# A ViT tower on one core: in the joined attention and routing stage, projections split into two rounded parts, ranks in one pass, and the steps of a chunk in another order

## Chip, core and metric

The kernel runs on one core of a Trainium2 chip, as one launch. The time is the device time of that core in microseconds (us). The core has five engines with instruction queues of their own, which work in order and meet at semaphores: TensorE (PE; its weight loads are shown apart as PEld), VectorE (DVE), ScalarE (ACT), GpSimd (POOL), and SyncE (SP), which only issues transfers. TensorE's clock is granted at one of two levels, 1.2 or 2.4 GHz; the profile gives it as a share, 1.00 or 0.50.

## The reference, cut to the part that the change touches

Five layers follow each other: token attention, gated linear attention, a mixture of experts, a second attention, a feed-forward net. Tokens are 4 x 3136 = 12544 rows of D = 192. The change lies in the second layer and in the routing half of the third:

```python
q = (elu(x @ Wq) + 1) * M ** -0.5          # M = 64; x is the layer-normed h
k = elu(x @ Wk) + 1
v = x @ Wv                                 # 192 x 192
log_f = log(clip(sigmoid(x @ Wf + bf), 1e-6))
log_f_cum = clip(cumsum(log_f, axis=1), -20, 20)
cum_kv = cumsum(exp(-log_f_cum)[..., None] * k[..., None] * v[..., None, :], axis=1)
numerator = einsum('blm,blmd->bld', q, exp(log_f_cum)[..., None] * cum_kv)
denominator = einsum('blm,blm->bl', q, exp_pos * cumsum(exp_neg * k, axis=1)) + 1e-6
h = h + layernorm(numerator / denominator) @ Wo
# experts: on layernorm(h)
routing = softmax(gelu(x @ w1 + b1) @ w2 + b2)      # 8 experts
topv, topi = top_k(routing, 2)                      # each row goes to two experts
```

## The kernel before

The tokens are worked in **chunks** of 448 rows (CH), each of four tiles of 112 rows (T, TPC = 4); there are NC = 28 chunks, seven to an image. `attend_route_phase` is the joined stage. One program loop over g = 0 to 30 carries four chunks at different depths: chunk g is attended to, chunk g+1 is projected, chunk g-1 gets its statistics, g-2 goes through the router's net, and g-3 gets its places in the experts' rows. The order of each engine is the order in which its block calls small functions, written out by hand; nothing else schedules it.

What one loop does for a chunk:

- **Into the attention.** ACT normalises four tiles into `xn` (`normalise`); PE transposes them into the PSUM tile `ptr` (`transpose_x`); DVE copies that to `xT` (`take_x`), 96 rows in two pieces. PE multiplies with the forget weights into `pff` and with query and key weights into `pqk` (`project`), and gives the values in `pvo` (`values`). These matmuls are f32, and each stands in the trace as two records.
- **Gates.** DVE takes `pff` (`gate_in`) and `pqk` (`elu_in`), ACT does exp, ln and the exp of the elu (`gate`), DVE scans (`scan`, which gives `cum`), ACT takes the exponential of `cum` (`decay`), and DVE makes `qt` and `kt` from it (`q_and_k`). With that the next chunk's loop can start.
- **Attention.** PE makes scores in `pat` and turns the keys into `pff` (`weights`); DVE masks them to `at` (`mask_weights`), ACT copies `ktok` (`keys_out`). In `attend` PE does three matmuls for each tile, the state `pst` among them, which ACT copies to `snap` (`states`). DVE divides (`sums_out`), takes statistics (`sums_stats`, `sums_aggr`), POOL makes the reciprocal root `rst` by a power (`factor`), PE transposes `hh` and multiplies with `wo` (`transpose_n`, `wo_out`), and DVE adds to `h` (`add_out`, which waits for `rst`), then the bias and the next norm's statistics (`add_bias`, `take_stats`; POOL: `factor_route`).
- **Routing.** ACT writes `xr` (`normalise_route`), PE transposes it (`transpose_r`), multiplies (`router`), ACT does the Gelu between two table loads (`take_hidden`), PE gives logits (`logits`), DVE and ACT the softmax (`softmax_head`, `take_ex`), DVE picks two experts (`choose`). PE counts in `rank` how many rows before each one went to its expert, with six f32 matmuls of 8 to 32 columns into the bank of `pqk`. DVE makes row numbers of it (`places`) and the gates (`share`). POOL writes each row to two places in HBM with eight indirect transfers (`scatter`), out of a ring of three `xr`.

`map_tiles` stands after the last loop and gives SP the ends of the experts' regions; SP then fills eight blocks of 448 rows with zeros, behind the semaphore `map_out`. The stage `tile_phase`, which reads these rows, begins when all engines and transfers of the joined stage are through.

During loops 0 and 1 ACT and DVE also split the experts' down weights in two (`high`, `split_low`).

Of the kernel before, what the change touches and what calls it, by code (L numbers as in the profile page):

```python
# [17 lines left out]
D = 192  # L18
# [24 lines left out]
E = 8  # L43
# [510 lines left out]
def attend_route_phase(nc, ins, h, bns, mean, rstd, minus, eye, held, gate, slot, shift, tile_e, tile_r, down,  # L554
# [3 lines left out]
    V1 = D + 1  # L558
    G3 = 3
    with ExitStack() as ctx:  # L560
        sb, ps, sem = allocator(nc, ctx, held)
        wqk = sb("wqk", [KC, 2, 128])
        wff = sb("wff", [KC, 2, 128])
        bff = sb("bff", [128, 1])
        wv = sb("wv", [KC, 2, D])
# [10 lines left out]
        xn = sb("xn2", [T, TPC, D])  # L576
        xT = sb("xT2", [KC, 2, CH])
# [21 lines left out]
        earlier = sb("before3", [T, T])  # L599
        number = sb("number3", [T, E])  # L600
        region = sb("region3", [T, E])
# [15 lines left out]
        sel = sb("sel3", [T, TPC, E])  # L617
# [10 lines left out]
        past = sb("past3", [1, 64, E])  # L628
        gone = sb("gone3", [1, 64, E])
# [3 lines left out]
        ptr = ps("ptr2", [KC, 2, 512])  # L633
# [7 lines left out]
        prk = pqk[0:T, 0:(TPC + 1) * E]  # L641

        names = ("w_in", "w_ready", "brow_mm", "minus_out", "xn_ready", "xtr_mm", "xT_out", "qk_mm", "ff_mm", "v_mm",
                 "v_out", "bias_out", "ntr_mm", "nT_out", "wo_mm", "h_out", "gate_in", "gate_out", "elu_in", "elu_out",
                 "cum_out", "dec_out", "qk_out", "ktr_mm", "ktok_out", "at_mm", "at_out", "st_mm", "snap_out",
                 "num_mm", "hhc", "hh_out", "agg_out", "rst_out", "dvec", "poolc")
        S = {n: sem(f"{n}_2") for n in names}
        route_names = ("w_in", "w_ready", "down_in", "high", "split", "cleared", "stat_out", "agg_out", "veps_out", "rstd_out", "off_out",
                       "half_out", "xr_ready", "rtr_mm", "rT_out", "r1_mm", "r1_out", "lg_mm", "mx_out", "lg_out",
                       "ex_out", "sel_out", "rank_mm", "rank_out", "idx_out", "dvec", "map_out", "filled")  # L650
# [9 lines left out]
        def _(sp):  # L660
            for dst, name in ((wqk, "wqk"), (wff, "wff"), (bff, "bff"), (wv, "wv"), (gam, "gam2"),
                              (bet, "bet2"), (sgn, "sgn"), (mask, "mask")):
                sp.dma_start(dst[:], ins[name]).then_inc(S["w_in"], 16)
            sp.dma_start(wo[:], ins["wo2"]).then_inc(S["w_in"], 16)
            for dst, name in ((w1[:], "w1"), (b1[:], "b1"), (w2[:], "w2"), (earlier[:], "before"),
# [9 lines left out]
            sp.wait_ge(R["map_out"], 3)  # L675
# [7 lines left out]
        def _(pool):  # L683
# [38 lines left out]
            for g in range(NC + 3):  # L722
                if here(g - 3):
                    scatter(g - 3, (0, 1))
                if here(g - 1):
                    factor_route(g - 1)
                if here(g - 3):
                    scatter(g - 3, (2, 3))
                if here(g):
                    factor(g)  # L730
                if g == 1:
                    pool.wait_ge(R["high"], 2)
                    pool.wait_ge(S["rst_out"], 2)
# [7 lines left out]
        def _(pe):  # L741
            pe.wait_ge(S["w_in"], 16 * 9)
# [30 lines left out]
            def values(g):  # L773
                if g:
                    pe.wait_ge(S["hh_out"], g)
# [1785 lines left out]
```

## Time and profile before

| | us |
|---|---|
| median of 3 runs (lowest, highest) | 2806.18 (2802.29, 2806.91) |
| the profiled execution | 2819.77 |
| its span, first to last instruction | 2817.9 |
| PE busy, of the span | 2376.4 (84%) |
| DVE busy | 1983.6 (70%) |
| ACT busy | 1514.0 (54%) |
| POOL busy | 999.0 (35%) |
| mean granted clock | 0.883 |

The joined stage begins at 854.8 us of the span (first instructions of its block), its first scores are at 880.90, its last ones at 1426.48, and the next block begins at 1499.11. The shares above are means over stages with different limits, so the stage is read on its own further down. A busy span of PE holds some latency behind its last column: the cost of one more matmul is read from the distance between starts.

### The profile page before, as it was taken

How to read it: one execution, taken by the hardware profiler on the slowest of the kernel's cores; microseconds unless marked ns; L12 is line 12 of the kernel's file. 1: busy time of each engine (PE TensorE's matmuls, PEld its weight loads, DVE VectorE, ACT ScalarE, POOL GpSimd, SP SyncE). 2: the span in 40 equal slices, each digit the busy share in tenths (PEclk: the TensorE clock that was granted, in tenths of full speed). 3: DMA queues.
4: the chain of work that ended last, by engine and by line, in shares of the span. 5: the costliest groups of instructions: out<-in, count | busy, mean ns of one | idle time of the engine just before them, and what ended most of it. 6: DMA issues, size and time to landing. Idle time of an engine off the chain costs nothing. (4 is left out here: it accounts for less than half of the span.)

```text
span 2817.9 us, 45185 instructions
## 1 busy us (share of the span) xinstructions
PE 2376.4 (84%) x14046; PEld 1704.3 (60%) x14047; DVE 1983.6 (70%) x5404; ACT 1514.0 (54%) x2636; POOL 999.0 (35%) x1024
## 2 busy tenths in 40 slices
PE   8999999999996999999964999926788885666665
PEld 4444444444444788888854999925677774444443
DVE  6777777777745788888853444447687877888886
ACT  2444444444442667676743665636565651777776
POOL 1100100100000355555552444468776720344343
PEclk9999999999997999999976999967687786677676
DMA  2000000000002011111116777731111100000000
GB/s 56 0 18 13 0 18 13 0 9 1 0 1 86 27 45 48 47 47 47 47 58 204 256 255 256 253 98 51 46 46 41 47 13 22 20 24 22 25 25 25
DMA packets 69334, 162.68 MB, mean 58 GB/s; under 512 B 13009, under 2 KB 32662, under 8 KB 68894
## 3 DMA queue, kind: packets, MB, share of 16 engines
q1 hardware_dynamic: 39618, 94.16, 10.2%
q0 software_dynamic: 21504, 44.99, 5.5%
q10 hardware_dynamic: 8064, 21.68, 2.5%
q8 instruction: 79, 1.29, 0.2%
q14 instruction: 69, 0.57, 0.1%
HBM read 63.87 MB, written 63.88 MB: 45 GB/s over the span
## 5 line engine op out<-in xcount | busy, mean ns | idle before, releaser
L418 DVE TENSOR_REDUCE pmax<-ppre 112x1 f32<-112x512 f32 x656 | 424.0, 686 | 161.6 <-PE ppre L260 161.5
L211 ACT ACTIVATE prob<-pscore 128x896 f32<-128x896 f32 x336 | 308.1, 917 | 421.9 <-PE pscore L293 421.9
L307 PE MATMUL pout<-prob,xkey 128*64 128x448 f32 x1344 | 327.5, 566 | 0.4 <-ACT prob L211 0.4
L718 POOL DMA_INDIRECT rows_in<-xr,idx x224 | 233.9, 1044 | 237.2 <-DVE idx L1189 180.2
L260 PE MATMUL ppre<-xh,yh 49*112 49x512 f32 x656 | 291.1, 446 | 7.8 <-DVE pmax L418 4.2
L260 PEld LDWEIGHTS ppre<-xh,yh 49*112 49x112 f32 x656 | 112.6, 172 | 239.1 <-issue 104.2
L1631 POOL DMA_INDIRECT yg<-rows_out,place x224 | 234.7, 1048 | 62.4 <-issue 62.1
L193 POOL CAST yh<-ynext 113x448 fp32r<-113x448 f32 x28 | 17.3, 616 | 666.4 <-DVE pmax L418 638.4
L293 PE MATMUL pscore<-yh,xh 49*128 49x448 f32 x700 | 241.1, 422 | 0.4 <-DVE yh L438 0.4
L2146 POOL TENSOR_TENSOR yg<-y,gout 112x512 f32<-112x512 f32 x112 | 141.2, 1271 | 265.5 <-DVE y L2379 265.5
L1481 POOL TENSOR_TENSOR zl<-z,zh 128x448 fp32r<-128x448 f32 x126 | 144.7, 1149 | 219.2 <-ACT zh L1447 209.8
L293 PE MATMUL pscore<-yh,xl 49*128 49x448 f32 x700 | 202.9, 364 | 0.0
L1395 PE MATMUL pz<-xth3b,wd 128*128 128x448 f32 x504 | 143.1, 386 | 0.0
L1501 DVE COPY yb<-py 112x384 f32<-112x384 f32 x126 | 70.2, 558 | 103.5 <-PE py L1409 103.4
L293 PE MATMUL pscore<-yl,xh 49*128 49x448 f32 x700 | 142.6, 364 | 0.0
L1709 PE MATMUL pqk<-xh,wh 128*128 128x448 f32 x168 | 78.8, 469 | 68.1 <-ACT junk L1852 56.0
L1409 PE MATMUL py<-uph,zh 128*112 x504 | 131.1, 260 | 1.2 <-POOL zl L1481 1.2
L1409 PE MATMUL py<-upl,zh 128*112 x504 | 131.7, 261 | 0.0
L2191 PE MATMUL pyt<-eyeb,yq 112*128 112x112 bf16 x448 | 41.7, 276 | 106.7 <-ACT yq L2267 106.7
L1409 PE MATMUL py<-uph,zl 128*112 x504 | 131.6, 261 | 0.0
L307 PEld LDWEIGHTS pout<-prob,xkey 128*64 128x64 f32 x1344 | 66.5, 135 | 105.6 <-issue 85.2
L293 PEld LDWEIGHTS pscore<-yh,xl 49*128 49x128 f32 x700 | 127.9, 187 | 0.7
(367 smaller groups left out, 6464.5 us busy)
## 6 DMA issues: line engine op xcount, KB each, us to landing
wd<-down SPq DMA_DIRECT2D x63, 512.0 KB, 3.0
xb<-rows_in SPq DMA_DIRECT2D x63, 448.0 KB, 3.6
rows_out<-yb ACTq DMA_DIRECT2D x63, 336.0 KB, 3.2
out<-ho SPq DMA_DIRECT2D x28, 336.0 KB, 2.8
rows_in<-zero SPq DMA_DIRECT2D x15, 448.0 KB, 5.3
rows_in<-xr,idx POOLq DMA_INDIRECT x224, 2.5
yg<-rows_out,place POOLq DMA_INDIRECT x224
xkey<-in_xkey SPq DMA_DIRECT2D x4, 800.0 KB, 6.8
```

Of the source, the lines that this page charges most:

```text
L211: nc.scalar.activation(prob[j % 3][:, :, :], pscore[j % 2][:, :, 0:CH], ACT.Exp).then_inc(exped, 1)
L260: pe.matmul(out[:, :], yh1[rows, q * T:(q + 1) * T], xh[b % 2][rows, block * 512:(block + 1) * 512], start=True, stop=True, tile_position= ...
L293: mm = pe.matmul(pscore[j % 2][:, i, 0:CH], x[b % 2][rows, keys], y[rows], start=(n == 0), stop=(n == 2), tile_position=(i * LO, 0))
L307: mm = pe.matmul(pout[i * LO:(i + 1) * LO, 0:CH], xkey[b % 2][:, 2 * j + i, :], prob[j % 3][:, i, :], start=(j == 0), stop=(i == 1 and j = ...
L418: nc.vector.reduce_max(pmax[:, q, 2 * block + half:2 * block + half + 1], bank(u, depth), AX.X).then_inc(pre_max, 1)
L718: nc.gpsimd.indirect_dma_start(rows_in, bass.IndirectOffsetOnAxis(ap=idx[r % G3][:, 2 * q + k:2 * q + k + 1], axis=0), xr[r % G3][:, q, :] ...
L1395: mm = pe.matmul(pz[m][:, 0:CH], wd[i][:, w, cols], x, start=(s_ == 0), stop=(s_ == 4))
L1409: mm = pe.matmul(py[i][:, q // 2, (q % 2) * D:(q % 2 + 1) * D], zz[i][m][:, cols], w[:, bass.ds(2 * e + m, 1), :], start=(m + n == 0), sto ...
L1481: nc.gpsimd.tensor_tensor(zl[i][m][:], z[m][:], zh[i][m][:].bitcast(F32), ALU.subtract).then_inc(S["zl_out"], 1)
L1631: nc.gpsimd.indirect_dma_start(yg[g % 2][:, q, k, :], None, rows_out, bass.IndirectOffsetOnAxis(ap=place[:, c:c + 1], axis=0)).then_inc(ga ...
L1709: mm = pe.matmul(pqk[m % 2][:, 0:CH], w, x, start=(n == 0), stop=(n == 4))
L2146: nc.gpsimd.tensor_tensor(yg[:, q, :], y[:, q, :], gout[:], ALU.mult).then_inc(S["yg_out"], 1)
```

## The change

It changes `attend_route_phase` alone, and the layout of its weights.

1. **Split projections.** The queries', keys', forget and value weights come as one tensor `wx`, 128 rows by two pieces by 448 columns. ACT rounds it to fp32r (`wxh`) and DVE takes the rest (`wxl`), once. For each chunk ACT copies `ptr` rounded (`high_x`: `xh`) and DVE takes what is left (`low_x`: `xl`, and rows 64 to 127 of the second piece). Each f32 product becomes three fp32r ones, in five matmuls where two f32 ones stood. `xn` has 256 columns, the last 64 a copy of columns 128 to 191, and two buffers.
2. **Ranks.** `rank` has fp32r operands (the counts are whole numbers) and writes into the bank of `pat`; it waits for the mask, and the router's product for DVE's `take_rank`, now apart from `places`.
3. **Order.** Scores come first in a loop of PE, the mask first in DVE's; `decay` stands ahead of `take_ex` and of both `values_out`; `wo_out`, `add_out` and `sums_stats` are in halves, `wo_out`'s second half and all of `add_out` a loop later; `choose` moves from loop r+2 to r+3, `scatter` from r+3 to r+4.
4. **End.** `map_tiles` comes before the last `share`, its two work tiles lie in `xrT` and `nT`, and SP's fills wait for its first result and not for its third.

The diff, cut to what is computed and waited for; the new order of calls stands below it.

```diff
 def project(g):
-    pe.wait_ge(S["xT_out"], g + 1)
-    if here(g - 4):
-        pe.wait_ge(R["rank_out"], g - 3)
-    for dst, w, done in ((pff, wff, "ff_mm"), (pqk, wqk, "qk_mm")):
-        for c in range(2):
-            mm = pe.matmul(dst[:, 0:CH], w[:, c, :], xT[:, c, :], start=(c == 0), stop=(c == 1))
+    pe.wait_ge(S["xL_out"], g + 1)
+    for dst, cols, done in ((pff, slice(128, 256), "ff_mm"), (pqk, slice(0, 128), "qk_mm")):
+        steps_ = ((wxh[:, 0, cols], xh[:, 0, :]), (wxh[:, 0, cols], xl[:]), (wxl[:, 0, cols], xh[:, 0, :]),
+                  (wxh[:, 1, cols], xh[:, 1, :]), (wxl[:, 1, cols], xh[:, 1, :]))
+        for n, (w, x) in enumerate(steps_):
+            mm = pe.matmul(dst[:, 0:CH], w, x, start=(n == 0), stop=(n == 4))
         mm.then_inc(S[done], 1)
 def values(g):        # for each of four tiles
-        for c in range(2):
-            mm = pe.matmul(pvo..., xT[:, c, q * T:(q + 1) * T], wv[:, c, :], ...)
+        steps_ = ((xh[:, 0, ts], wh[:, 0]), (xh[:, 0, ts], wl[:, 0]), (xl[:, ts], wh[:, 0]),
+                  (xh[:, 1, ts], wh[:, 1]), (xh[:, 1, ts], wl[:, 1]))
+def high_x(g):        # ACT
+    act.wait_ge(S["xtr_mm"], g + 1)
+    nc.scalar.copy(xh[:, :, :], ptr[:, :, 0:CH]).then_inc(S["xH_out"], 1)
-def take_x(g):        # DVE
-    dve.wait_ge(S["xtr_mm"], g + 1)
-    nc.vector.tensor_copy(xT[:, :, :], ptr[:, :, 0:CH]).then_inc(S["xT_out"], 1)
+def low_x(g):
+    dve.wait_ge(S["xH_out"], g + 1)
+    nc.vector.tensor_tensor(xl[:], ptr[:, 0, 0:CH], xh[:, 0, :].bitcast(F32), ALU.subtract)
+    nc.vector.tensor_tensor(xh[64:128, 1, :], ptr[64:128, 1, 0:CH], xh[64:128, 1, :].bitcast(F32),
+                            ALU.subtract).then_inc(S["xL_out"], 1)
-prk = pqk[0:T, 0:(TPC + 1) * E]
+prk = pat[:, 0:(TPC + 1) * E]
-sel = sb("sel3", [T, TPC, E])
+sel = sb("sel3", [T, TPC, E], F32R)
 def rank(r):
     pe.wait_ge(R["sel_out"], r + 1)
+    if here(r + 3):
+        pe.wait_ge(S["at_out"], r + 4)
 def attend(g, tiles):  # tiles 0, 1
-        pe.wait_ge(S["h_out"], g)
+        pe.wait_ge(S["h_half"], g)
-sp.wait_ge(R["map_out"], 3)
+sp.wait_ge(R["map_out"], 1)
```

DVE in a middle loop, before, from the mask on (`xT` is `take_x`, `den` begins `sums_out`):

```order
L1106 TENSOR_TENSOR at<-pat,mask 112x448
L1123 TENSOR_TENSOR h<-h,brow 112x768
...
L1130 BN_STATS bns<-h 112x6 x4
L1134 BN_AGGR agg3r<-bns 112x2 x4
L1045 COPY xT<-ptr 96x896
L1052 TENSOR_SCALAR den<-pvo 112x2 x2
...
L1102 TENSOR_TENSOR kt<-elu,dec 64x448
L1115 SCALAR_TENSOR_TENSOR h<-pvo,rst,h 112x192 x4
L1162 TENSOR_REDUCE total<-ex 112x4
```

And in the changed kernel, again from the mask (`total` to `sel` is `choose`, `xl` and `xh` are `low_x`):

```order
L1151 TENSOR_TENSOR at<-pat,mask 112x448
L1159 SCALAR_TENSOR_TENSOR h<-pvo,rst,h 112x192 x2
L1206 TENSOR_REDUCE total<-ex 112x4
...
L1216 TENSOR_TENSOR sel<-pick 112x32
L1159 SCALAR_TENSOR_TENSOR h<-pvo,rst,h 112x192 x2
L1167 TENSOR_TENSOR h<-h,brow 112x768
...
L1231 TENSOR_TENSOR run<-pat,run 112x8
L1086 TENSOR_TENSOR xl<-ptr,xh 128x448
L1087 TENSOR_TENSOR xh<-ptr,xh 64x448
L1095 TENSOR_SCALAR den<-pvo 112x2 x2
```

`add_out` has moved from behind `q_and_k` to behind the next mask, in halves with `choose` between them; the statistics of `hh` (not shown) lie in halves after `elu_in` and after `q_and_k`.

PE around the place where one loop ends and the next begins, before (`wo` is `wo_out`, `kt` the scores of the next chunk):

```order
L859 MATMUL pat<-w_3,r 112x8 x4
L778 MATMUL pvo<-wv,xT 112x192 x8
L829 MATMUL pvo<-wo,nT 112x192 x8
L842 MATMUL ptr<-eye,xr_2 96x112 x8
L787 MATMUL pat<-qt,kt 112x112 x4
L791 MATMUL pff<-eye,kt 112x128 x4
L868 MATMUL pqk<-sel,before 112x8
```

And in the changed kernel (of the 20 matmuls of `values` the last two are shown):

```order
L790 MATMUL pvo<-wxh,xh 112x192
L790 MATMUL pvo<-wxl,xh 112x192
L843 MATMUL pvo<-wo,nT 112x192 x4
L799 MATMUL pat<-qt,kt 112x112 x4
L803 MATMUL pff<-eye,kt 112x128 x4
L856 MATMUL ptr<-eye,xr_1 96x112 x8
L843 MATMUL pvo<-wo,nT 112x192 x4
L820 MATMUL pst<-vt,ktok 128x193
```

The scores stand between the two halves of `wo_out`, and the ranks no longer stand ahead of `attend`'s first half: they follow the transposes of the next chunk.

ACT in the changed kernel, from the key copy to the copies of the values (before, the four `snap` stood in one row behind `ktok`, and `xn` was the last of the loop):

```order
L998 COPY ktok<-pff 112x4x64
L938 ACTIVATE xn_1<-h,minus,rstd 112x192
L961 COPY xrT<-ptr 96x896
...
L938 ACTIVATE xn_1<-h,minus,rstd 112x192
L943 COPY xn_1<-xn_1 112x4x64
L1004 CAST xh<-ptr 128x896
L1009 COPY snap<-pst 128x193 x2
...
L975 COPY nT<-ptr 96x896
L994 ACTIVATE dec<-cum,sgn 128x448
L988 COPY vt<-pvo 112x2x192 x2
```

`decay` (`dec`) is ahead of both copies of the values; it stood between them.

## Rows read from the trace of the kernel before

**Rows 1.** Windows: stretch, length, busy us of PE, PEld, DVE, ACT, POOL, clock, DMA.

```profile
880.90:948.42 67.52, 57.42 (x302) 48.91 (x303) 42.31 (x116) 32.84 (x64) 8.39 (x11) 0.87 0.00 1
948.42:1426.48 478.06, 471.81 (x2972) 396.68 (x2971) 397.12 (x1586) 326.27 (x623) 263.42 (x288) 1.00 0.15 47
1426.48:1499.11 72.63, 31.84 (x162) 24.91 (x160) 27.66 (x159) 19.76 (x31) 34.64 (x38) 0.63 0.32 102
```

**Rows 2.** Waits of DVE, 1100:1299.2, ten loops: us in total, times, longest.

```profile
DVE elu L1081 <- PE pqk L770: 8.2, 10, 0.8
DVE den L1052 <- PE pvo L811: 7.6, 10, 0.8
DVE h L1115 <- PE pvo L829: 6.4, 20, 0.5
DVE qt L1101 <- ACT dec L972: 5.8, 10, 0.6
```

**Rows 3.** Timeline of PE in one loop: start us, length us, what; ranks, then projections.

```profile
1208.85 0.36 PE L868 MATMUL pqk<-sel,before 112*112 112x8 f32 x2
...
1210.05 0.57 PE L806 MATMUL pst<-vt,ktok 112*128 112x193 f32 x2
...
1216.39 1.67 PE L770 MATMUL pff<-xT,wff 96*128 96x448 f32 x4
...
1219.40 0.93 PE L820 MATMUL ptr<-eye,hh 112*96 112x112 f32 x8
```

**Rows 4.** Timeline of PE, the loop before: values, output product, router's transposes.

```profile
1200.97 2.83 PE L778 MATMUL pvo<-wv,xT 96*112 96x192 f32 x16
1203.64 2.76 PE L829 MATMUL pvo<-wo,nT 96*112 96x192 f32 x16
1206.57 0.97 PE L842 MATMUL ptr<-eye,xr 112*96 112x112 f32 x8 [0.17 <-ACT xr L935]
```

**Rows 5.** Timeline of PE in the experts' stage: fp32r matmuls, 192 and 448 columns.

```profile
1640.07 0.26 PE L1409 MATMUL py<-uph,zh 128*112 x1
1640.17 0.26 PE L1409 MATMUL py<-uph,zl 128*112 x1
...
1641.56 0.99 PE L1395 MATMUL pz<-xth3b,wd 128*128 128x448 f32 x4
1642.39 0.37 PE L1395 MATMUL pz<-xtl3b,wd 128*128 128x448 f32 x1
```

**Rows 6.** Experts' stage, the split of a transposed tile: ns, least, median, most.

```profile
L1436 ACT CAST xth3b<-ptr3b x63: 899/907/912, 1506.0 to 1838.7; 128x896 fp32r<-128x896 f32 x63
L1491 DVE TENSOR_TENSOR xtl3b<-ptr3b,xth3b x63: 615/625/626, 1507.0 to 1839.7; 128x448 fp32r<-128x448 f32 x63
L1492 DVE TENSOR_TENSOR xth3b<-ptr3b,xth3b x63: 627/627/628, 1507.6 to 1840.3; 64x448 fp32r<-64x448 f32 x63
```

**Rows 7.** Timeline of all engines in one loop: scan, exponential, root, copy, table load.

```profile
1220.21 1.15 DVE L1086 TENSOR_TENSOR_SCAN cum<-ones_scan,tail,gate 128x448 f32<-128x448 f32 x1
...
1222.97 0.66 ACT L972 ACTIVATE dec<-cum,sgn 128x448 f32<-128x448 f32 x1
...
1223.67 1.04 POOL L700 TENSOR_TENSOR rst<-veps,mhalf 112x4 f32<-112x4 f32 x1
...
1233.19 1.05 DVE L1045 COPY xT<-ptr 96x896 f32<-96x896 f32 x1
...
1237.16 1.28 ACT L945 ACT_TABLE_LOAD   x1
```

**Rows 8.** Timeline of the stage's end, DVE and SP: the map and the fills.

```profile
1474.82 0.15 DVE L1202 CAST fill<-run 1x8 int32<-1x8 f32 x1
...
1479.70 0.21 DVE L1218 SCALAR_TENSOR_TENSOR tile_r<-gone_t,which_e 1x64 int32<-1x64 f32 x1
...
1481.13 11.81 SPq L678 DMA_DIRECT2D rows_in<-zero  x8
```

**Rows 9.** Timeline of PE in the stage's second loop: a long gap.

```profile
905.31 0.57 PE L806 MATMUL pst<-vt,ktok 112*128 112x193 f32 x2 [3.83 <-DVE at L1106]
```

More of the change, by code:

```diff
@@ L892, in _ @@
                     transpose_x(g + 1)
+                if here(g - 3):
+                    rank(g - 3)
                 if here(g):
@@ L938, in take_r @@
                 act.wait_ge(R["rtr_mm"], r + 1)
[L939 removed]
+                nc.scalar.copy(xrT[:, :, :], ptr[0:KC, :, 0:CH]).then_inc(R["rT_out"], 1)
             def take_hidden(r):
@@ L1008, in _ @@
                 if here(g + 1):
-                    values_out(g + 1, 0)
+                    decay(g + 1)
+                    for i in range(2):
+                        values_out(g + 1, i)
                 if here(g - 2):
                     take_ex(g - 2)
-                if here(g + 1):
-                    decay(g + 1)
-                    values_out(g + 1, 1)
                 if here(g - 1):
                     normalise_route(g - 1)
-                if here(g + 2):
-                    normalise(g + 2)
                 if g < 2:
@@ L1233, in _ @@
                 if here(g - 1):
-                    add_bias(g - 1)
+                    add_out(g - 1, 0)
+                if here(g - 3):
+                    choose(g - 3)
+                if here(g - 1):
+                    add_out(g - 1, 1)
+                    add_bias(g - 1)
+                    take_stats(g - 1)
+                if here(g - 3):
+                    take_rank(g - 3)
+                if here(g + 1):
+                    low_x(g + 1)
+                if here(g):
+                    sums_out(g)
+                if here(g - 1):
+                    offset(g - 1)
                 if here(g - 3):
                     places(g - 3)
-                    share(g - 3)
-                if here(g - 1):
-                    take_stats(g - 1)
-                if here(g + 1):
-                    take_x(g + 1)
-                if here(g):
-                    sums_out(g)
-                    sums_stats(g)
+                if g == NC + 2:
+                    map_tiles()
                 if here(g + 1):
@@ L1258, in _ @@
                 if here(g):
-                    add_out(g)
-                if here(g - 2):
-                    choose(g - 2)
+                    sums_stats(g, (2, 3))
+                    sums_aggr(g)
+                if here(g - 3):
+                    share(g - 3)
                 if g < 2:
                     split_low(g)
-            map_tiles()
 def expert_phases(nc, ins, h, bns, mean, rstd, minus, eye, held, scattered):
```

223 lines of the change are left out of this document (132 added, 91 removed).

## The prediction

> **What bounds the kernel now.** I read the stretches of the joined stage first. From the fourth loop's scores to the last loop's, 24 loops take 478.06 us, 19.92 each, at a clock of 1.00, and PE is busy for 471.81 of them [rows 1]. Then I ask who waits. PE waits once in a loop, 0.17 us for ACT's `xr` [rows 4]; so its queue holds 19.75 us of work, and PE bounds the loop. DVE waits 28.0 us in ten loops, 2.8 in each, at four places, three of them for PE [rows 2]; its queue needs 19.92 - 2.8 = 17.1. That is the second bound, and it is near. The rest of the stage is no steady flow: the first three loops take 67.52 us at a clock of 0.87, and 72.63 us pass from the last scores to the next block at 0.63, with no engine busy for half of it [rows 1].
>
> **PE's queue after the change.** The distance between starts is what counts.
> - Projections: two banks take 1219.40 - 1216.39 = 3.01 us now [rows 3]. Ten fp32r matmuls of 448 columns take the place, at (1642.39 - 1641.56)/4 = 0.207 us each [rows 5]: 2.07. Saved: 0.94.
> - Values: 1203.64 - 1200.97 = 2.67 us now [rows 4]. Twenty fp32r matmuls of 192 columns, each with 112 columns of weights to load, at 0.10 us (0.098 in the longer run of them) [rows 5]: 1.96. Saved: 0.71.
> - Ranks: 1210.05 - 1208.85 = 1.20 us for twelve records [rows 3], six records after: 0.60 if a record costs the same 0.10. Saved: 0.60.
> - The transposes stay eight, with 128 weight columns for 96: nothing either way, as they are counted by the 112 columns that move.
>
> Sum 2.25; PE's queue needs 17.5 us.
>
> The Trainium skill, TensorE: Matmul & The Clock Gate, section "Back-to-back issue gap", gives N/2.4 + 2.5 ns for an isolated gap, 82 ns for 192 columns, and says itself that it counts too little where weights are loaded; the row has 98, and the row decides. By the formula PE's queue would be 0.3 shorter, which changes nothing below, since PE's queue alone is not what I expect to bind.
>
> **DVE's queue.** `take_x` goes, 1.05 us [rows 7]; `low_x` comes, 0.625 + 0.627 [rows 6]: +0.20, so 17.3 us. Moved steps cost what they cost. The waits are what is left to find, since PE (17.5) and DVE (17.3) are now almost equal, and neither can be late for the other without the loop getting longer. ACT gains the rounded copy, 0.91 [rows 6], and a copy of 256 elements, some 0.4; it was busy 326.27/24 = 13.6 us a loop [rows 1] and stays at 15. Not a bound by itself, but its order matters.
>
> **The longest chains from loop to loop**, walked with the new order:
> - *PE to ACT to DVE to ACT to PE.* PE's queue from the scores to the end of the router's product is 17.5 less what stands behind it: projections 2.07, transposes of `hh` and logits 1.49 (from 1219.40 to the values, which start 19.92 after 1200.97 [rows 3, 4]), values 1.96, half of `wo_out` 1.4 (2.76 is the whole, latency included [rows 4]). That leaves 10.6, and 10.8 with the latency to ACT. Gelu, exp and ln, 448 columns each, under 0.66 apiece as the exponential of `cum` is, and a table load of 1.28 between them [rows 7]: 3.1, so 13.9. The scan with its two followers: the clip and ACT's start lie within 1222.97 - 1220.21 = 2.76 now [rows 7], of which some 0.8 is the aggregate that moves away and the queue ahead of `decay` on ACT; 1.9, so 15.8. `decay` 0.66, one copy of values some 0.5, half of `wo_out` 1.4: 18.4.
> - *DVE to POOL to DVE.* `sums_aggr` is now late in the loop, and POOL's two steps, of which the power takes 1.04 [rows 7], lie between it and `add_out`, about 1.4 with both. DVE has `share` and the mask to do meanwhile, about 1.1. So this wait adds 0.3: 17.3 + 0.3 and some tenths for the breaks between halves, 17.9. POOL's scatters stand a loop later and have 6 us of slack; they don't come between, in the steady loops.
> - *ACT's own row*: `decay`, values, `normalise_route`, `ktok`, four `xn`, `xrT`, two `snap`, the pad, `high_x`, and from there DVE to the next `decay`: about 17.3, under the others.
>
> Both ends of the unknown: no handoff costs anything more, 17.6; each of DVE's present waits stays at half, 17.3 + 1.4 and the POOL wait 0.3, 19.0. I take **18.4**, the longest chain, since the first end asks that three queues of nearly equal length never wait. 24 loops x (19.92 - 18.4) = **36.5 us**.
>
> **The first loops and what is ahead of them.** Ahead of the first scores the projections run at half clock: twice 3.0 = 6.0 us before, twice 2.0 = 4.0 after; `decay` no longer waits for both value copies. Against it stand the split of `wx` and one more handoff, 0.9. I take -3, between 0 and -5; the row of transfers gets one tensor more of 448 KB, which the transposes hide, as they wait for `wo`'s algebra. In the first three loops PE stood 3.83 us for a mask that was behind the split of `down` [rows 9]. ACT now reaches its part of that split 1.9 us sooner in either loop, as four `xn` no longer precede it, and the loops have no `choose` and no ranks yet. They took 67.5; at 18.4 with two stalls of 1.5 they take 58. **-9**, between -5 and -12. Together **-12**.
>
> **The drain.** Two things. (a) SP starts its fills at the map's first result; now it starts 1.2 us after the third, which comes 1479.70 - 1474.82 = 4.9 us after the first [rows 8]. (b) `factor` and `factor_route` of the last chunks no longer stand behind the scatters of a chunk nearer, so the last router starts sooner: some 5 us; its ranks take half, and at half clock that is 1.2 more. The fills then would begin some 11 us sooner and take their 17 us. What comes next as late: POOL's 32 indirect transfers of the last four chunks, 1.25 us each, 40 us; they begin 11 us after the last scores and have two stops for the roots: 57 us, and 59 when they land. They share the DMA queues with the fills, which then end near 62. Before it was 72.63. **-10**, between -4 and -13.
>
> **Sum.** 36.5 + 12 + 10 = 58.5 us. The profiled execution, 2819.77, goes to 2761; it stands 13.6 above the median, so the median goes from 2806.18 to **2748**. Later stages have the same instructions.
>
> **Rivals.**
> - *The waits stay* (19.0 us a loop). For it: an in-order queue that is 94% full is released late by each of its partners, and every order of these calls moves a wait. It decides when DVE waits over 1.4 us a loop. 24 x 0.9 = 22, with 22 from the ends: 2762.
> - *Nothing waits* (17.6). For it: the order was made for these chains, and the walks above may hold slack twice. 24 x 2.3 = 55, with 22: 2729.
> - *The clock falls, and the change ends slower.* In the steady loops PE never stands over 0.17 us and the clock is 1.00; in the first three it stood for 3.83 [rows 9] and the mean was 0.87 [rows 1]. Now PE will stand about 0.9 us in every loop, ahead of the values' product with `wo` and the scores, and its fp32r work streams fewer columns in the same time. If the clock fell for part of every loop, PE's 17.5 us become 17.5/c plus 0.9. That equals the break-even loop, 19.92 + 22/24 = 20.8, at c = 0.88; at c = 0.83 it is 22.0, so 24 x 2.1 = 50 lost against 22 won at the ends: 2834. Against it: the experts' stage is all fp32r, and by its rows keeps its distances of 0.098 and 0.207 us [rows 5], and the gaps are a quarter of those that went with low clock. The Trainium skill has a rule for this, TensorE: Matmul & The Clock Gate, "A second HAM failure mode: psum-queue depth-cycling": short idle spells between groups of matmuls make the clock swing. By that rule this change pays; these rows show the swing only with gaps of several us.
> - *The ends give nothing*: fills and scatters slow each other, and the first loops stall as before. Loops alone: 2770.
>
> **How the numbers follow.** Forecast 0.56 (2736 to 2758), waits stay 0.19, ends give nothing 0.06, nothing waits 0.11, clock falls 0.08. The range must hold eight in ten: 2732 to 2782 takes in the forecast, both middle cases, and the near edge of the fast one; the clock case and the fastest stay out. A measurement here tells about 0.2%, 5.6 us, from no change. Faster by more than that: 0.90; within: 0.03, the edge between waits and clock; slower: 0.07.
>
> **What would show it.** The steady loop, from scores to scores, at 18.4, with DVE busy about 16.8 of it and PE 17.3; the clock at 1.00 there; `py`-like distances of 0.10 in the values; DVE's longest wait at `add_out` for POOL, some tenths; ACT's copies of the values directly behind `decay`, with PE waiting 0.5 to 1 us for the first. The fills begin about 43 us after the last scores, and the next block about 62. Wrong if DVE's `low_x` waits for ACT (then the handoff is on the chain), if the router's product waits for `take_rank`, or if the clock leaves 1.00 in the steady loops.

## The result

| | before, us | changed, us | ratio, 95% interval |
|---|---|---|---|
| median (lowest, highest), 4 runs each | 2804.23 (2802.08, 2806.91) | 2788.59 (2784.79, 2790.76) | 0.994 [0.9925, 0.9954] |

The changed kernel is 15.6 us shorter, where the prediction had 58, and 6.6 us above the top of its range. The same program was then run on later occasions, each with the kernel before beside it. A "visit" is one such occasion: several kernels on one chip, one after the other. On two visits it took 2788 us again, on another 2747.16 (2742.86 to 2749.5), a ratio of 0.9794 [0.9777, 0.981], which is the predicted time. So there are two results to explain, and the traces of both stand side by side from here: that of the first result, called **late**, and that of the fast visit, called **prompt**.

The stretches that answer to [rows 1]: stretch, length, busy us of PE, PEld, DVE, ACT, POOL, clock, DMA share. First late, then prompt.

```profile
880.05:937.38 57.33, 48.63 (x304) 44.08 (x305) 41.49 (x106) 36.35 (x69) 8.58 (x9) 0.91 0.00 1
937.38:1407.03 469.65, 422.61 (x2973) 379.30 (x2972) 408.77 (x1606) 354.51 (x665) 255.51 (x284) 1.00 0.16 47
1407.03:1481.49 74.46, 33.14 (x153) 25.44 (x152) 30.41 (x173) 22.01 (x38) 40.22 (x44) 0.62 0.34 105
```

```profile
879.68:937.47 57.79, 49.00 (x304) 43.98 (x305) 41.49 (x106) 36.19 (x69) 8.57 (x9) 0.91 0.00 1
937.47:1370.37 432.90, 414.25 (x2973) 379.25 (x2972) 402.49 (x1606) 356.77 (x668) 243.47 (x284) 1.00 0.17 51
1370.37:1440.17 69.80, 31.51 (x153) 24.02 (x152) 30.34 (x173) 20.90 (x34) 39.24 (x44) 0.62 0.36 112
```

The next block starts at 1481.49 late and at 1440.17 prompt (1499.11 before). The first three loops are alike. The 24 loops differ: 469.65/24 = 19.57 us late, 432.90/24 = 18.04 prompt, 19.92 before.

Who waits in ten loops (us in total, times, longest). Late, PE and then ACT:

```profile
PE ptr L856 <- ACT xr L957: 11.1, 10, 1.2
PE pvo L843 <- ACT vt L988: 6.2, 10, 0.6
...
ACT vt L988 <- remote: 11.5, 10, 1.2
```

Prompt, PE and then DVE (all that DVE waits, but for 0.5 us):

```profile
PE pvo L843 <- ACT vt L988: 7.9, 10, 1.1
...
DVE h L1159 <- POOL rst L705: 3.7, 10, 0.4
```

"remote" means that the profile shows no engine's work ending just before the wait does. The place, in the timeline of one late loop (ACT), start us and length us:

```profile
1207.75 0.67 ACT L994 ACTIVATE dec<-cum,sgn 128x448 f32<-128x448 f32 x1 [0.57 <-issue]
1208.33 0.46 ACT L988 COPY vt<-pvo 112x384 f32<-112x384 f32 x1
1209.91 0.48 ACT L988 COPY vt<-pvo 112x384 f32<-112x384 f32 x1 [1.12 <-remote]
1210.29 0.23 ACT L971 ACTIVATE ex<-lg 112x32 f32<-112x32 f32 x1
1210.42 1.85 ACT L953 ACTIVATE xr<-h,minus,rstd 112x192 f32<-112x192 f32 x4
```

and of PE and POOL in the same loop:

```profile
1206.65 1.20 POOL L723 DMA_INDIRECT rows_in<-xr,idx  x1 [0.30 <-issue]
1208.16 0.94 POOL L723 DMA_INDIRECT rows_in<-xr,idx  x1 [0.30 <-issue]
```

```profile
1208.05 0.26 PE L790 MATMUL pvo<-wxl,xh 128*112 128x192 f32 x1
1208.93 1.52 PE L843 MATMUL pvo<-wo,nT 96*112 96x192 f32 x8 [0.62 <-ACT vt L988]
1210.29 0.95 PE L799 MATMUL pat<-qt,kt 128*112 128x112 f32 x8
1211.08 0.60 PE L803 MATMUL pff<-eye,kt 128*112 128x128 f32 x4
1212.76 0.97 PE L856 MATMUL ptr<-eye,xr 112*96 112x112 f32 x8 [1.08 <-ACT xr L957]
```

The last product of the values ends at 1208.05 + 0.26 = 1208.31, and ACT, which waits for nothing else, copies that half at 1209.91, 1.6 us later. The trace also records each step of a semaphore, and it has this one at 1209.89: the signal itself is late, not ACT. ACT then does `ex` and `xr` 1.1 us later than it could, and PE stands 1.08 us at the router's transposes. The prompt trace has the same instructions in the same order, and here the two copies are one piece with no wait between them (ACT, then PE):

```profile
1205.62 0.67 ACT L994 ACTIVATE dec<-cum,sgn 128x448 f32<-128x448 f32 x1 [0.57 <-DVE cum L1135]
1206.20 0.84 ACT L988 COPY vt<-pvo 112x384 f32<-112x384 f32 x2
...
1208.94 0.40 ACT L957 COPY xr<-xr 112x256 f32<-112x256 f32 x1
```

```profile
1206.81 1.52 PE L843 MATMUL pvo<-wo,nT 96*112 96x192 f32 x8 [0.76 <-ACT vt L988]
1208.17 0.95 PE L799 MATMUL pat<-qt,kt 128*112 128x112 f32 x8
...
1209.40 0.97 PE L856 MATMUL ptr<-eye,xr 112*96 112x112 f32 x8
```

ACT's last copy of `xr` ends at 1209.34 here, just ahead of the transposes at 1209.40.

GpSimd's first scatter starts at 949.32 in the late trace, in the fourth loop. No step of PE's semaphores is recorded late before it. The fourth loop still takes 18.02 us, and those from the fifth on 19.5 to 19.8.

### The profile page after: what moved, and what is told of

Same layout as the page of the kernel before. It is cut to its first block and busy times, and to the rows that moved or that the text cites. A ratio compares the mean times of both kernels' runs of the same rounds, so it can differ in the third digit from the quotient of the medians.

```text
span 2788.9 us, 45419 instructions
## 1 busy us (share of the span) xinstructions
PE 2293.3 (82%) x14046; PEld 1665.0 (60%) x14047; DVE 2000.3 (72%) x5437; ACT 1550.6 (56%) x2693; POOL 996.8 (36%) x1024
```

## The experiments

### First visit: the wait for xr, the scatters, and the two halves of the change

**TensorE's order.** In `block.tensor` the half of `wo_out` goes ahead of the transposes that wait:

```diff
+                if here(g - 1):
+                    wo_out(g - 1, (2, 3))
                 if here(g - 2):
                     transpose_r(g - 2)
-                if here(g - 1):
-                    wo_out(g - 1, (2, 3))
```

> One edit to the changed kernel: on TensorE, wo_out(g-1, (2, 3)) is written ahead of transpose_r(g-2), so that the transposes that wait for ACT's xr (1.08 us at 1212.76 in the changed kernel) come one step, 1.3 us of matmuls, later. Theory A (the loop is 19.6 us because TensorE waits for xr, which ACT writes last in its loop): the wait of ptr for xr falls from about 1.1 to under 0.2 us a loop, the steady loop from 19.6 to 18.6 us, the kernel by 24 x 1.0 = 24 us, to about 2765. Rival B (the loop is held by the chain VectorE - rst on GpSimd - add_out, and TensorE's wait only mirrors it): the wait reappears at once behind it, as a wait of the states for at or h, the loop stays within 0.2 us of 19.6 and the time within 5 us of the changed kernel's 2788.6. Either way the update of the second half of the values still comes 1.6 us after the last matmul.

Measured: 2764.09 us, ratio 0.9842 [0.9825, 0.986]; 18.73 us a loop. The number is theory A's, but the reason is not: nothing is late in this trace, so there was no wait of 1.1 us for `xr` to take away. What the order does is worse than nothing. ACT and then PE, ten loops:

```profile
ACT xrT L961 <- PE ptr L856: 12.5, 10, 1.3
...
PE pst L820 <- ACT snap L1009: 7.1, 10, 1.0
```

The later transposes make ACT's `xrT` late, the copies of the states stand behind that in ACT's queue, and PE waits 0.7 us for them. I could say so only once the unchanged program had run prompt.

**The scatters' place.** In `block.gpsimd` and in VectorE's loop:

```diff
-                if here(g - 4):
-                    scatter(g - 4, (0, 1))
                 if here(g - 1):
                     factor(g - 1)
                 if here(g - 4):
-                    scatter(g - 4, (2, 3))
+                    scatter(g - 4, range(TPC))
...
-                if here(g - 1):
-                    offset(g - 1)
                 if here(g - 3):
                     places(g - 3)
...
                     elu_out(g + 1)
+                if here(g - 1):
+                    offset(g - 1)
```

> One edit to the changed kernel: on GpSimd all eight scatters of a chunk stand between factor and factor_route, so none is issued while the values are multiplied (in the changed kernel four of them, at 1204.10 to 1209.10, surround the values' last matmul at 1208.05); VectorE's offset stands behind the scan, since rstd now comes about 4 us later. Theory A (a scatter issued beside the values delays the semaphore update of their second half, which ACT sees 1.6 us late): ACT's wait at the second vt copy, 1.15 us a loop, falls under 0.3 us, and the loop by 0.5 to 1.0 us, since xr is written so much earlier and TensorE waits for it: about 2770. Rival B (the lateness belongs to TensorE, to the wait that follows the last values matmul, whatever GpSimd does): the wait stays at 1.1 us and the time stays within 5 us of the changed kernel's. Rival C: offset now waits for factor_route and the loop grows by the wait, 0.5 us or more, which the row of minus would show.

Measured: 2748.97 us, 0.9785 [0.9769, 0.9802]; 431.54/24 = 17.98 us a loop, no late update. At the time it looked like theory A. It was not: the visit was a prompt one.

**Arithmetic alone.** All calls back in the old order (of each engine, with the ranks in `pqk`), the new products kept:

```diff
-        prk = pat[:, 0:(TPC + 1) * E]
+        prk = pqk[0:T, 0:(TPC + 1) * E]
...
+                if here(g - 2):
+                    transpose_r(g - 2)
                 if here(g):
                     weights(g)
-                if here(g - 2):
-                    transpose_r(g - 2)
-                if here(g - 1):
-                    wo_out(g - 1, (2, 3))
+                if here(g - 3):
+                    rank(g - 3)
...
-                    wo_out(g, (0, 1))
+                    wo_out(g, range(TPC))
```

> The changed kernel with every engine's calls, the bank of the ranks, their waits and the scatters put back into the order of the kernel before: what is left of the change is its arithmetic alone, split projections and values, one-pass ranks, and the high and low copies of x on ACT and VectorE. Theory A (the arithmetic shortens only TensorE's row, which waits 1.5 us more a loop for ACT and VectorE, and the added copy on ACT, 0.9 us, and on VectorE, 0.3 us, lie on the path that bounds the old order): the loop stays at 19.9 to 20.3 us, and the kernel at 2800 to 2812 us, no faster than before. Rival B (TensorE bounded the old order, and 2.2 us of it are gone): loop 18.5 to 19 us, kernel about 2775 to 2785.

**Order alone.** All calls as in the changed kernel, the products in float32:

```diff
-                    steps_ = ((wxh[:, 0, cols], xh[:, 0, :]), (wxh[:, 0, cols], xl[:]), (wxl[:, 0, cols], xh[:, 0, :]),
-                              (wxh[:, 1, cols], xh[:, 1, :]), (wxl[:, 1, cols], xh[:, 1, :]))
+                    steps_ = ((wx[:, 0, cols], xh[:, 0, :]), (wx[0:64, 1, cols], xh[0:64, 1, :]))
```

> The changed kernel's order with the old arithmetic: projections, values and ranks as plain float32 products in two pieces of 128 and 64 rows, one copy of x on VectorE in two pieces (as long as the two subtractions) in the place of the high copy on ACT and the low one on VectorE, and no padding of xn on ACT. TensorE's row is 2.2 us a loop longer and ACT's 1.3 us shorter than in the changed kernel. Theory A (TensorE's row is what the order needs short): it would wait for nothing and the loop be its own row, 19.8 us and more, kernel 2795 to 2805. Rival B (the order alone already gives what the change gave, since the loop is held by links): loop 19.5 us, kernel within 5 us of 2788.

Measured: arithmetic alone 2792.82 us, 0.9954 [0.9936, 0.9972]; order alone 2859.91, 1.017 [1.0147, 1.0193]. Their 24 loops:

```profile
944.62:1416.30 471.68, 428.26 (x2973) 376.79 (x2971) 402.98 (x1609) 352.30 (x671) 248.82 (x288) 1.00 0.16 48
```

```profile
950.04:1472.33 522.29, 517.84 (x2972) 379.42 (x2971) 400.80 (x1608) 331.24 (x621) 250.50 (x285) 1.00 0.14 42
```

Arithmetic alone: 19.65 us a loop. It takes 1.9 us of work off PE (19.75 before; here the loop less 1.77 of waits, 17.88) and 0.27 off the loop, and all of the rest comes back as waits (in ten loops PE 7.4 us for `ktok` and 6.5 for `xr`, DVE 9.5 for `xh`): theory A in kind, though it ended 7 us under the range I gave. Order alone: 21.76 a loop with PE busy for nearly all of it. That is more than the 19.8 of theory A, and its timeline of PE says why (projections, then values):

```profile
1157.02 1.86 PE L775 MATMUL pff<-xh,wx 128*128 128x448 f32 x4
1158.81 1.97 PE L775 MATMUL pqk<-xh,wx 128*128 128x448 f32 x4
1160.70 0.97 PE L829 MATMUL ptr<-eye,hh 112*96 112x112 f32 x8
...
1162.23 4.11 PE L785 MATMUL pvo<-wx,xh 128*112 128x192 f32 x16
1166.27 1.55 PE L838 MATMUL pvo<-wo,nT 96*112 96x192 f32 x8
```

The same sixteen records of values take 1166.27 - 1162.23 = 4.04 us in pieces of 128 and 64 rows, and 2.67 in pieces of 96 and 96 [rows 4]; the projections 3.68 against 3.01 [rows 3]. With the old pieces the loop would be about 21.76 - 1.37 - 0.67 = 19.7, an estimate that was not run. So the arithmetic alone is worth 0.27 us a loop as measured, the order alone about 0.2 by that estimate (with the pieces that were run it costs 1.84), and both together 1.88 on a prompt visit. It looks as if PE's work had to shrink for the order to pay, and the order to change for the smaller work to show.

### Second visit: four edits that should have told causes apart

**Both edits of above.** 

> Both single edits together: the changed kernel with wo_out(g-1, (2, 3)) ahead of transpose_r(g-2) on TensorE, and with all eight scatters between factor and factor_route on GpSimd and offset behind the scan on VectorE. Alone they gave 18.75 us a loop (TensorE waited 0.7 us for the states' copy instead of for xr, since ACT's xrT came late) and 17.96 us (TensorE waits 0.7 us for vt and for nothing else). Theory A (each removes the same wait, TensorE's for xr, and the scatters' edit removes its cause): no gain is added, the loop stays at 18.0 us or is longer, since the later transposes of xr make xrT late again: 17.9 to 18.7 us, kernel 2748 to 2768. Rival B (two separate waits): the gains add, loop 17.3 us, kernel 2730.

Measured: 2762.6 us, 0.9828 [0.9808, 0.9849], 18.73 us a loop. The swap's cost is there, nothing else.

**`xr` ahead of the second half, on ACT.**

```diff
                     decay(g + 1)
-                    for i in range(2):
-                        values_out(g + 1, i)
+                    values_out(g + 1, 0)
                 if here(g - 2):
                     take_ex(g - 2)
                 if here(g - 1):
                     normalise_route(g - 1)
+                if here(g + 1):
+                    values_out(g + 1, 1)
```

> One edit to the changed kernel: on ACT, the copy of the values' second half stands behind normalise_route, so ACT no longer waits for that half (1.15 us a loop) ahead of ex and xr. Everything else, GpSimd's scatters included, stays. Theory A (ACT's wait for the second half, and xr behind it, is what TensorE's wait for xr comes from): xr is ready 1.6 us earlier, TensorE's wait for it goes, the loop falls to 18.0 to 18.5 us, kernel 2750 to 2765. Rival B (the late update is only a mirror of another hold): loop stays at 19.6 us, kernel at 2785 to 2790. The update of the second half itself: if it is tied to the scatters at that place it is still 1.6 us late in the trace, and now costs nothing; if it is tied to TensorE's wait for xr it is prompt, as it was once wo_out stood ahead of the transposes with the scatters where they were.

**A semaphore of its own for the second half.**

```diff
-                        mm.then_inc(S["v_mm"], 1)
+                        mm.then_inc(S["v2_mm" if q // 2 else "v_mm"], 1)
...
-                act.wait_ge(S["v_mm"], 2 * g + i + 1)
+                act.wait_ge(S["v2_mm" if i else "v_mm"], g + 1)
```

> The changed kernel with the second half of the values on a semaphore of its own, in place of the second step of the one that both halves use: nothing else moves. If the lateness belongs to two updates of one semaphore from matmuls 1 us apart, ACT's wait at the second vt copy goes from 1.15 to under 0.2 us and the kernel from 2788 to about 2765. If it belongs to the place in the loop (scatters beside the values, or TensorE's wait for xr), it stays: 1.1 us a loop, 2788 within 5 us.

**`offset` alone behind the scan** (the second part of the scatters' diff). 

> The changed kernel with VectorE's offset behind the scan and GpSimd as it was: the half of the scatters' experiment that is not the scatters. offset is 0.15 us and stands ahead of the spots and indices, so the scatters start some 0.1 us earlier. If the scatters' place was the cause of the gain (2749), this stays at 2788 within 5 us, with ACT's wait for the second half at 1.1 us. If the offset was the cause, it gives most of 40 us: 2750 to 2765.

Measured: 2748.09 us, 0.9781 [0.9762, 0.9799]; 2744.4, 0.9771 [0.9748, 0.9795]; 2747.11, 0.9776 [0.9755, 0.9798]. All three loops are 18.03 or 18.04 us, none has a late update. Three unlike edits with one result, one of them without any effect on the order of work, is the sign that none of them is the cause. What they had in common was the visit.

### Third visit: the changed kernel again

> The changed kernel as it is, once more, beside the next two. Five small edits of it gave 18.0 us a loop and 2744 to 2749 us, two of them edits that move nothing in the loop (a semaphore of its own for the second half of the values; offset 3 us later on VectorE), and in none is the update of the second half late. Theory A (the lateness is a state of the chip or of the day on which the changed kernel was timed): 2748 within 5 us, loops of 18.0 us, no wait of ACT for the second half. Rival B (it belongs to this exact program): 2788 within 5 us, loops of 19.6 us from the fifth on, ACT's second vt copy waits 1.1 us.

**One unused semaphore more.**

```diff
-"v_mm",
+"v_mm", "spare",
```

> The changed kernel with one semaphore more that nothing uses, named behind the values' own, so that the numbers of all that follow move up by one as in the kernel where the second half had a semaphore of its own. If two updates of one semaphore are what is late, this one stays at 2788; if the lateness hangs on a coincidence of this exact program (numbers of semaphores, places of instructions in memory) or on the chip, it gives 2748 like the kernel with its own semaphore.

**The fills behind the whole map**, in the kernel with a semaphore of its own:

```diff
-            sp.wait_ge(R["map_out"], 1)
+            sp.wait_ge(R["map_out"], 3)
```

> The kernel with a semaphore of its own for the second half (2744 us on one chip), and the fills of the drain back behind the whole map: SyncE waits for its third step, some 5 us after the first. In that kernel the fills are issued from 47.1 us after the last scores and the next block starts at 69.5 us after them, while the last eight scatters go beside the fills. Theory A (fills and scatters share the DMA engines, and the stage ends when the sum of their bytes has passed): the block starts under 2.5 us later, kernel 2744 to 2747. Rival B (the fills are a serial end of the stage): 5 us later, 2749.

Measured: 2787.72 us, 0.9932 [0.9912, 0.9953]; 2787.61, 0.9932 [0.9906, 0.9958]; 2785.43, 0.9918 [0.9896, 0.994]. All three are late, with ACT's 1.15 us a loop at `vt` and 19.6 us a loop. The third one has, in its loops, the very instructions of the kernel that took 2744.4 us on the second visit, so the program doesn't decide it. It also has the second half of the values on a semaphore of its own and is late all the same, so two updates of one semaphore are not what is late.

The third one also answers a question on the drain. The last scatter, the fills and the next block, in the unchanged program and with later fills:

```profile
1464.63 0.94 POOL L723 DMA_INDIRECT rows_in<-xr,idx  x1 [0.30 <-issue]
```

```profile
1456.32 13.45 SPq L683 DMA_DIRECT2D rows_in<-zero  x8
1479.17 0.38 SPq L1395 DMA_DIRECT2D downb<-in_downb  x1
```

```profile
1464.85 0.94 POOL L723 DMA_INDIRECT rows_in<-xr,idx  x1 [0.31 <-issue]
```

```profile
1461.43 12.32 SPq L683 DMA_DIRECT2D rows_in<-zero  x8
1479.93 0.38 SPq L1395 DMA_DIRECT2D downb<-in_downb  x1
```

The fills begin 5.1 us later and the block 0.8 later. That is within the spread of the changed kernel as it is, whose block stands 13.6 to 15.0 us behind the end of its last scatter in its four traces. So its block does not follow the fills. It keeps a distance from the last scatter: 13.6 and 14.1 us here, 13.9 in the prompt trace, 14.3 in the late one, 13.3 to 16.3 in all twenty traces; from the first fill the distance runs from 18.0 to 26.3. In the kernel before it was 14.5: its last scatter, by the line below, ends at 1484.66, and the block starts at 1499.11.

```profile
1483.72 0.94 POOL L718 DMA_INDIRECT rows_in<-xr,idx  x1 [0.30 <-issue]
```

In that kernel the fills may have ended just as late. Its block came 18.0 us after the first fill, the shortest of the twenty, where the prompt trace has 22.7; and its transfers went on until 2.8 us ahead of the block. The DMA share is 0.00 for the last 7.0 us in the late trace and for the last 6.5 in the prompt one. What those 14 us consist of is not shown.

### Fourth visit: the changed kernel beside three of its edits

> The changed kernel once more, on one chip with three of its edits. It gave 2788 us on two occasions with late updates of the values' second half (19.6 us a loop); its five small edits gave 2744 to 2749 us with prompt ones (18.0 us), all on two chips on which the changed kernel itself has not run. Theory A (the chip): all four kernels of this call agree, all prompt at 2744 to 2750 or all late at 2785 to 2790. Rival B (the program): this one is late and 40 us longer than the two beside it.

> The second half of the values on a semaphore of its own, as in e7_own_sem (2744 us, prompt), beside the changed kernel on the same chip. Theory A (the chip): the same loop as the changed kernel's in this call, within 0.1 us. Rival B (the program): 18.0 us a loop whatever the chip; but with only the fills' wait changed the same program was late on another chip (2785 us), which speaks for A.

> All eight scatters between factor and factor_route, as in e2_scatter_late (2749 us), beside the changed kernel on the same chip. If this chip shows the late update in the changed kernel, this run tells whether scatters beside the values are needed for it: then 18.0 us a loop and prompt here against 19.6 us there. If the chip shows no late update, both are at 18.0 us and this run says only that the place of the scatters is worth nothing.

> ACT's copy of the second half behind normalise_route, as in e6_xr_first (2748 us), beside the changed kernel on the same chip. If this chip shows the late update, it should be late here too (1.6 us) and cost nothing, since ACT does ex and xr in that time: 18.1 us a loop against 19.6 us. If it shows none, both are at 18.0 us.

Measured: 2747.16 us, 0.9794 [0.9777, 0.981]; 2749.1, 0.9797 [0.978, 0.9813]; 2743.46, 0.9781 [0.9765, 0.9797]; 2744.87, 0.9791 [0.9773, 0.9809]. All prompt. Theory A holds in so far as the kernels of one visit agree. The chip has the same number as on the second visit.

### Fifth visit: a late one, with two edits

> The changed kernel once more beside two of its edits. So far it has been late (19.6 us a loop, 2788 us) on one chip and prompt (18.06 us, 2747 us) on another, and every kernel that shared a call agreed with it. This run says which kind this chip is: 2785 to 2790 or 2744 to 2750.

> All eight scatters between factor and factor_route. On a chip that is late: if the scatters beside the values are needed for the lateness, 18.0 us a loop and 2745 to 2750 us; if not, 19.5 us and 2785 or more, with ACT's wait of 1.1 us for the second half. On a chip that is prompt: 18.0 us, as before, and nothing is learned of it.

> ACT's copy of the second half behind normalise_route. On a chip that is late: the second half comes 1.6 us late but ACT does ex and xr in that time, so TensorE's wait for xr goes: 18.1 us a loop, 2745 to 2752 us; if the hold is elsewhere, 19.6 us. On a chip that is prompt: 18.05 us, as before.

Measured: 2788.61 us, 0.9937 [0.9911, 0.9963]; 2957.89, 1.0537 [1.0501, 1.0572]; 2786.82, 0.9926 [0.99, 0.9952]. The chip has the number of the second and fourth visits, which were prompt: so it isn't the chip for good, but something that holds through a visit. The kernel before has medians of 2804.23, 2808.10 and 2806.16 us on late visits and of 2808.47, 2810.41 and 2806.57 on prompt ones: in time it doesn't feel it. Whether its signals are late too isn't known, since its one trace has the marks of a prompt one (see the end of this section).

The scatters' edit is the telling run. All eight scatters now stand beside the states, the transposes of `x` and the ranks. Its loops, 17.98 us on the first visit, are 26.5 here. The window holds the first 22 of the 24, and the rows below it tell what waits in seven of them:

```profile
936.93:1519.82 582.89, 446.41 (x2723) 385.49 (x2723) 368.85 (x1472) 329.21 (x617) 214.40 (x256) 0.83 0.11 34
```

```profile
PE pst L818 <- ACT snap L1007: 43.3, 7, 6.2
DVE pos L1226 <- remote: 41.3, 7, 6.0
ACT xh L1002 <- remote: 29.3, 7, 4.7
...
ACT snap L1007 <- remote: 17.4, 7, 3.4
```

One of these loops, all engines' rows that matter:

```profile
1146.26 0.93 PE L763 MATMUL ptr<-eye,xn 112*128 112x112 f32 x8
...
1150.33 0.91 ACT L1002 CAST xh<-ptr 128x896 fp32r<-128x896 f32 x1 [3.32 <-remote]
...
1151.91 0.95 POOL L723 DMA_INDIRECT rows_in<-xr,idx  x1 [0.30 <-issue]
...
1154.57 0.19 DVE L1226 TENSOR_TENSOR pos<-pat,run 112x32 f32<-112x32 f32 x1 [6.01 <-remote]
1154.62 0.32 ACT L1007 COPY snap<-pst 128x193 f32<-128x193 f32 x1 [3.38 <-remote]
```

The transposes end at 1147.2, and ACT sees it at 1150.3. The ranks and the third state end at about 1148, and VectorE and ACT see them at 1154.6, after the eighth scatter. This loop is 27 us, and the clock is 0.83 over the window, with PE standing 6 us in each. The values' signals, which were late in the changed kernel on the same visit, are prompt here, where no scatter stands beside them. So on a late visit the signal that tells another engine of a finished matmul can come some us late while GpSimd issues scatters. It was 1.6 us in the changed kernel, where they stand in fours, and up to 6.9 us (1147.69 to 1154.55, for the ranks) with eight in a row. Two kernels are no rule for how it grows.

With `xr` first the second half of the values is still signalled 1.6 us late, by the trace's record of the semaphore, and costs nothing, as expected. But the loop stays at 19.56 us, outside the 18.1 of the expectation: a second signal, that of the transposes of `x`, is now later as well, and ACT waits 1.9 us for it (eight of ten loops):

```profile
ACT xh L1004 <- remote: 15.6, 8, 2.0
```

In the changed kernel's late trace that one is 0.5 us late in about half of the loops and 1.8 us late in one. So an order that hides one late signal does not cure the kernel: the next one is not far.

**What marks a late trace.** The records of the semaphores tell more than the waits. I count the steps of PE, ACT and DVE that have no record within 0.06 us of the end of their instruction, be it late or missing. In the seven late traces these are 274 to 388 of about 1860 while GpSimd issues its scatters, 115 to 125 of about 740 in a later stage, where GpSimd issues 224 indirect gathers, and none of 5600 elsewhere. In the 13 other traces it is none, none or up to 3, and none. So in every late trace the late and missing steps keep to the stages of GpSimd's indirect DMAs. In the later stage it costs nothing that shows: from the first gather to the last it takes 411.3 to 414.0 us late, and 411.1 to 415.7 in the prompt traces of the changed kernel and its edits. The trace of the kernel before has none of 742 in that stage, whose instructions are the same, so it is a prompt trace. And since records are missing too, the recording itself may take part: every time on record comes with a span and a clock, so no execution without any recording can be set against them.

## Why the prediction was wrong, and where it was right

The prediction's number is met on a prompt visit, 2747 for 2748, in part by luck, and missed on the visit that gave the result. Step by step, with the prompt trace for the mechanism:

- *PE's queue 17.5.* 18.04 less the 0.79 that it waits: 17.25. From start to start a matmul took 0.10 us in the values and 0.20 in the projections. Right, 0.25 too high.
- *DVE's queue 17.3, waits some tenths for POOL.* Busy 402.49/24 = 16.8, as said, and 0.37 a loop of waiting at `add_out` for `rst`. The wait is right. The queue, loop less waits as the prediction counts it, is 18.04 - 0.42 = 17.6: 0.3 too low.
- *The longest chain, 18.4.* PE waits at one place, 0.79 us for the first copy of the values behind `decay`, which the prediction named with 0.5 to 1. The chain was 0.36 too long: 24 x 0.36 = 8.7 us that came on top.
- *The clock.* 1.00 in the steady loops although PE stands 0.8 us in each (late: 1.7 in each), so the rival fell. It showed in one experiment, 0.83 with gaps of 6 us.
- *First loops and what is ahead.* Three loops 57.79 us (57.33 late) for 58. Ahead of the first scores 1.2 us (0.85 late) for 3. The first projection started 1.5 us later than before (870.70 for 869.16), where the sum allowed 0.9. And the scores wait for the copy that makes the ranks' ones, a step that the sum left out: `kt` is done at 879.13 and the scores start at 879.68, which costs some 0.4 us.
- *The drain, -10.* Wrong. It gave 72.63 - 69.80 = 2.8 us prompt, and took 1.8 more late. The fills began 47.1 us after the last scores (54.6 before, 43 said), but that isn't what failed. The walk had the last scatter at 57 us, near the measured 55.9, and gave it 2 us to land. The next block came 14 us after it, a distance that the trace of before already has. The last chunk's indices come hardly sooner after the last scores than before (45.7 us for 47.6), and the last scatter ended 58.2 us after them before, so there was little to win. Fills and scatters also go through two queues in the trace, q1 and q0, not through shared ones; they share the 16 engines.
- *The sum.* Prompt: 1.2 + 9.7 + 45.2 + 2.8 = 58.9 for 58.5. The total is right by luck, because two errors cancel, 8.7 more from the loops and 7.2 less from the drain.
- *The step that failed for the result* is the one on the longest chains. Every handoff was priced by rows of before, about 0.2 us at most, and the wait of the transposes for `xr` was not walked at all, though `xr` is PE's only wait in [rows 4]: the walk to `xr` ends 0.06 us ahead of the transposes even when signals are prompt. On a late visit one signal comes 1.6 us late, ACT is 1.1 late at `xr`, PE stands 1.1, and 1.53 x 24 = 37 us of the loops' 45 are gone. With the drain's 4.7 that is the whole difference of 41 us between the two traces' blocks. Of the 1.53 PE's waits account for 1.2; the rest lies in spans that count as busy (422.61 for 414.25 us). No row of before shows such a lateness, and none of the rivals was this one. "The waits stay" gave its sign in the late trace, DVE waiting 1.8 us a loop for over 1.4, but it had 19.0 us a loop and 2762, and its reason was a full queue and not a late signal. The prediction's own sign of being wrong, `low_x` waiting for ACT, also came there (2.8 us in ten loops, none in the prompt trace).

Open: what makes a visit late, whether the recording takes part, and why the kernel before isn't slower on a late visit. Its scatters, too, stand beside the states and the projections. One difference is that it has no split or one-pass products in that stage, while each late signal that a wait shows here came from such a product or from one of its neighbours. Neither arithmetic alone nor order alone was run on a late visit, which would have told.

## What to carry to other kernels

A change that leaves PE (17.3), DVE (17.6) and the longest chain (18.0) within a microsecond of each other leaves little room for one late signal. That is argued, not tested: PE had as little room before. So price the chains once with each handoff at its usual 0.2 us and once with a microsecond or two more beside indirect DMAs, and put the second into the range. When unlike edits all give the same gain, run the unedited kernel beside them before believing any. And before counting on an earlier start of something at a stage's end, look in the old trace for what the next block keeps its distance from.

## What of the hardware was not expected

- The signal of a finished matmul can reach ACT or DVE 1.6 to 6.9 us late beside GpSimd's indirect DMAs, and in no other stage of these traces. On a late visit every changed kernel traced there had it. It came on three of six visits and was absent in the same program on the others. In its worst form it cost 209 us (2748.97 against 2957.89 for one kernel).
- The same 16 float32 records of values take 4.04 us in pieces of 128 and 64 rows and 2.67 us in pieces of 96 and 96.
- The next block starts 13.3 to 16.3 us after the end of the last scatter's issue in all twenty traces, with fills that start 3.6 to 11.1 us ahead of that end.
